# A graph network layer pair in one program: the expert rows transposed by a DMA from SBUF to SBUF instead of by TensorE

## The reference, cut to what matters

```python
logits = jnp.einsum('bsd,de->bse', input, Wg)
probs = jax.nn.softmax(logits, axis=-1)
top_vals, top_idx = jax.lax.top_k(probs, TOP_K)
...
h = jnp.einsum('ebsd,edh->ebsh', xm, W1) + b1[:, None, None, :]
h = jax.nn.relu(h)
y = jnp.einsum('ebsh,ehd->ebsd', h, W2) + b2[:, None, None, :]
out = jnp.sum(y * jnp.moveaxis(scores, -1, 0)[..., None], axis=0)
```

## Time and profile before

| | us |
|---|---|
| median of 3 runs | 2253.19 |
| lowest and highest of them | 2250.86, 2257.51 |
| the profiled execution, its span | 2275.1 |
| TensorE busy in it | 2087.9 (92%) |
| first work of the expert stage (first gather issued) | at 2065.9 |
| last accumulating write issued | at 2266.8 |

### The profile page before, as it was taken

The page is one execution under the profiler, slowest core; times in us unless marked ns, Lnnn a source line. Parts: engine busy times, 40 slices in busy tenths (PEclk is TensorE's granted clock), DMA queues, the critical chain, the costliest instruction groups (busy, mean ns, idle before and its releaser), DMA issues.

```text
span 2275.1 us, 41642 instructions
## 1 busy us (share of the span) xinstructions
PE 2087.9 (92%) x16528; PEld 1432.7 (63%) x16528; DVE 1235.5 (54%) x2230; ACT 752.7 (33%) x1097; POOL 1083.7 (48%) x797
## 2 busy tenths in 40 slices
PE   5969999999999989979999999999999998976997
PEld 5526446455447967754445577757887788874665
DVE  5871551554486789984634632545545534275332
ACT  4242453553564434440031322411211122051332
POOL 5456778678774420004621783025324425423554
PEclk9989999999999999988999999999999999987999
DMA  3311323232445420023000012300100000376886
GB/s 136 84 32 22 84 61 81 67 84 67 103 128 129 131 82 20 20 109 97 19 19 28 21 45 75 97 28 29 56 28 28 30 17 29 117 288 206 152 155 107
DMA packets 106982, 176.89 MB, mean 78 GB/s; under 512 B 31057, under 2 KB 76248, under 8 KB 100542
## 3 DMA queue, kind: packets, MB, share of 16 engines
q1 hardware_dynamic: 89966, 145.63, 20.4%
q0 software_dynamic: 16848, 28.90, 7.5%
HBM read 120.82 MB, written 53.49 MB: 77 GB/s over the span
## 4 chain that ended last, share of the span: by engine, by line
PE 77%; DVE 10%; issue 5%; POOL 4%; ACT 3%; DMA 2%; DVEq 0%; POOLq 0%; ACTq 0%; SPq 0%; another core or an unknown queue 0%
PE ps L487 19%; PE ps L489 19%; PE ps L490 19%; PE pt L697 4%; DVE RB L778 3%; PE ps L681 3%; PE pt L681 1%; PE pt L875 1%; ACT SR L740 1%; PE pt L1107 1%; PE ps L1126 1%; PE ps L1127 1%; PE ps L1128 1%; PE pt L472 1%; DVE RB L1760 1%
## 5 line engine op out<-in xcount | busy, mean ns | idle before, releaser
L487 PE MATMUL ps<-WR,RB 128*128 128x256 f16 (+2 forms) x2280 | 640.7, 281 | 11.0 <-POOL WR L1421 3.7
L489 PE MATMUL ps<-WR,RB 128*128 128x256 f16 (+2 forms) x2280 | 640.0, 281 | 0.1
L490 PE MATMUL ps<-WR,RB 128*128 128x256 f16 (+2 forms) x2280 | 639.7, 281 | 0.0
L487 PEld LDWEIGHTS ps<-WR,RB 128*128 128x128 f16 x2280 | 223.9, 98 | 58.5 <-issue 6.7
L1421 POOL TENSOR_TENSOR WR<-WR 128x2048 f16<-128x2048 f32 (+2 forms) x40 | 188.5, 4712 | 146.7 <-ACT WR L594 145.3
L487 PE MATMUL ps<-RB,WR 128*128 128x512 f16 (+1 forms) x720 | 244.4, 339 | 10.1 <-DVE RB L439 7.4
L490 PEld LDWEIGHTS ps<-WR,RB 128*128 128x128 f16 x2280 | 223.7, 98 | 43.6 <-issue 0.6
L489 PEld LDWEIGHTS ps<-WR,RB 128*128 128x128 f16 x2280 | 224.2, 98 | 41.1 <-issue 0.8
L490 PE MATMUL ps<-RB,WR 128*128 128x512 f16 (+1 forms) x720 | 244.3, 339 | 0.0
L489 PE MATMUL ps<-RB,WR 128*128 128x512 f16 (+1 forms) x720 | 244.3, 339 | 0.0
L1414 POOL TENSOR_TENSOR WR<-WR,units 128x3072 f32<-128x3072 f32 (+2 forms) x18 | 81.4, 4522 | 339.7 <-PE ps L487 334.7
(11 more groups left out here) (338 smaller groups left out, 4013.4 us busy)
## 6 DMA issues: line engine op xcount, KB each, us to landing
WR<-in_w_moe SPq DMA_DIRECT2D x64, 256.0 KB, 3.5
moe_split<-WR SPq DMA_DIRECT2D x128, 128.0 KB, 1.8
RB<-moe_split SPq DMA_DIRECT2D x8, 2048.0 KB, 13.7
WR<-in_w_mix SPq DMA_DIRECT2D x12, 1024.0 KB
WR<-in_w_mix SPq DMA_DIRECT2D x8, 1536.0 KB
RB<-in_x SPq DMA_DIRECT2D x18, 512.0 KB, 6.1
WR<-in_w_out SPq DMA_DIRECT2D x8, 1024.0 KB
RB<-counts SPq DMA_DIRECT2D x10, 640.0 KB, 4.8
```

The costliest lines, as they stand in the source:

```text
L487: m = nc.tensor.matmul(o, ah, bh, start=(k == 0), stop=False)
L489: nc.tensor.matmul(o, ah, bl, start=False, stop=False)
L490: m = nc.tensor.matmul(o, al, bh, start=False, stop=(k == n - 1))
```

## The change

TensorE no longer transposes the gathered rows, and ACT and DVE no longer copy them. In their place SP issues one transposing DMA a tile, from `xg` to `xT`, when the gather has landed and, from the fifth tile on, when `up` of the tile four before has read its buffer. `xT` gets four buffers. `pt`, which held the transposed rows, is used as a second set of banks for `up` and `down`, by odd and even tiles, so that both wait for the copy two tiles back instead of that of the tile before. The gather waits for the transposing DMA that read its buffer, where it waited for TensorE.

```diff
-        xT = [WR(24576 + 4096 * j, F16, 2, KD, 128) for j in range(2)]
+        xT = [WR(24576 + 4096 * j, F16, 2 * KD, 128) for j in range(2)] + [
+            SR(S1 + 8192 + 4096 * j, F16, 2 * KD, 128) for j in range(2)]
+        NX = len(xT)
...
+        def up_bank(t):
+            return (ps[:, 0, :] if t % 2 == 0 else pt[:, 0, 0, :])[:, 0:HE]
+
+        def down_bank(t, c):
+            return ps[:, 2 + c, :] if t % 2 == 0 else pt[:, 1, c, :]
...
-            def rows_turn(t):
-                pe.wait_ge(xg_loaded[t % NG], 16 * (t // NG) + 16)
-                if t >= 2:
-                    pe.wait_ge(xt_hi, t - 1)
-                    pe.wait_ge(xt_lo, t - 1)
-                for b in range(2):
-                    for k in range(KD):
-                        m = nc.tensor.transpose(pth[t % 2][:, b, k], xg[t % NG][:, b, k * 128:(k + 1) * 128], ident_h)
-                m.then_inc(xt_done, 1)
-
...
                 pe.wait_ge(blk_loaded[min(t, NE - 1)], 16)
-                pe.wait_ge(xt_hi, t + 1)
-                pe.wait_ge(xt_lo, t + 1)
-                if t >= 1:
-                    pe.wait_ge(u_hi, t)
-                    pe.wait_ge(u_lo, t)
+                pe.wait_ge(xt_loaded[t % NX], 16 * (t // NX) + 16)
+                if t >= 2:
+                    pe.wait_ge(u_hi, t - 1)
+                    pe.wait_ge(u_lo, t - 1)
...
-                if t >= 1:
-                    pe.wait_ge(y_out[c], t)
+                if t >= 2:
+                    pe.wait_ge(y_out[c], t - 1)
...
-            rows_turn(0)
             up(0, e)
-            rows_turn(1)
             hidden_turn(0)
             for t in range(MT):
-                if t + 2 < MT:
-                    rows_turn(t + 2)
                 if t + 1 < MT:
                     up(t + 1, e1)
...
-                nc.scalar.activation(xT[t % 2][:, 0], pth[t % 2][:, 0], ACT.Copy).then_inc(xt_hi, 1)
...
-                    pool.wait_ge(xt_done, t - NG + 1)
+                    pool.wait_ge(xt_loaded[(t - NG) % NX], 16 * ((t - NG) // NX) + 16)
...
             block_load(7)
+            for t in range(MT):
+                sp.wait_ge(xg_loaded[t % NG], 16 * (t // NG) + 16)
+                if t >= NX:
+                    sp.wait_ge(u_done, t - NX + 1)
+                sp.dma_start_transpose(out=xT[t % NX], in_=xg[t % NG].rearrange("p b n -> p (b n)")
+                                       ).then_inc(xt_loaded[t % NX], 16)
...
-                v.tensor_copy(xT[t % 2][:, 1], pth[t % 2][:, 1]).then_inc(xt_lo, 1)
```

More of the change, by code:

```diff
@@ L285, in build_program @@
         pt = ctx.enter_context(nc.psum_tensor("pt", [128, 2, 2, 512], F32))
-        pth = [pt[:, s, :, :].rearrange("p b c -> p (b c)").bitcast(F16).rearrange("p (b k n) -> p b k n", b=2, k=KD)
-               for s in range(2)]
         psh16 = ps[:, 1, :].bitcast(F16)
@@ L364, in build_program @@
         xg_loaded = [sem(f"xg_loaded{j}") for j in range(NG)]
-        xt_done, xt_hi, xt_lo = sem("xt_done"), sem("xt_hi"), sem("xt_lo")
+        xt_loaded = [sem(f"xt_loaded{j}") for j in range(NX)]
         u_done, u_hi, u_lo = sem("u_done"), sem("u_hi"), sem("u_lo")
@@ L1114, in up @@
                 pe.wait_ge(blk_loaded[min(t, NE - 1)], 16)
-                pe.wait_ge(xt_hi, t + 1)
-                pe.wait_ge(xt_lo, t + 1)
-                if t >= 1:
-                    pe.wait_ge(u_hi, t)
-                    pe.wait_ge(u_lo, t)
+                pe.wait_ge(xt_loaded[t % NX], 16 * (t // NX) + 16)
+                if t >= 2:
+                    pe.wait_ge(u_hi, t - 1)
+                    pe.wait_ge(u_lo, t - 1)
                 def w(at):
                     return WB[:, bass.ds(e, 1), at:at + HE].rearrange("p a n -> p (a n)")
-                o, x = ps[:, 0, 0:HE], xT[t % 2]
+                o, x = up_bank(t), xT[t % NX]
                 nc.tensor.matmul(o, pick_e[:, 0, t:t + 1].to_broadcast([128, 128]), b1s, start=True, stop=False)
                 for k in range(KD):
-                    nc.tensor.matmul(o, x[:, 0, k], w(k * HE), start=False, stop=False)
-                    nc.tensor.matmul(o, x[:, 0, k], w(2048 + k * HE), start=False, stop=False)
-                    m = nc.tensor.matmul(o, x[:, 1, k], w(k * HE), start=False, stop=(k == KD - 1))
+                    nc.tensor.matmul(o, x[:, k], w(k * HE), start=False, stop=False)
+                    nc.tensor.matmul(o, x[:, k], w(2048 + k * HE), start=False, stop=False)
+                    m = nc.tensor.matmul(o, x[:, KD + k], w(k * HE), start=False, stop=(k == KD - 1))
                 m.then_inc(u_done, 1)
@@ L1339, in up_hi @@
                     act.wait_ge(ht_done, t - 1)
-                nc.scalar.activation(hr[t % 2][:, 0], ps[:, 0, 0:HE], ACT.Relu, scale=1.0 / (XS * WS)).then_inc(u_hi, 1)
+                nc.scalar.activation(hr[t % 2][:, 0], up_bank(t), ACT.Relu, scale=1.0 / (XS * WS)).then_inc(u_hi, 1)
             def hidden_hi(t):
@@ L1352, in y_first @@
                     act.wait_ge(summed[0], 16 * (t - 2))
-                nc.scalar.activation(yo[t % 3][:, 0:512], ps[:, 2, :], ACT.Copy,
+                nc.scalar.activation(yo[t % 3][:, 0:512], down_bank(t, 0), ACT.Copy,
                                      scale=sc[:, t:t + 1]).then_inc(y_out[0], 1)
             act.wait_ge(sc_ready, 1)
-            rows_hi(0)
             up_hi(0)
-            rows_hi(1)
             hidden_hi(0)
             for t in range(MT):
-                if t + 2 < MT:
-                    rows_hi(t + 2)
                 if t + 1 < MT:
```

14 lines of the change are left out of this document (3 added, 11 removed).

## The result

| | before | after |
|---|---|---|
| median, us | 2254.78 (4 runs) | 2298.02 (4 runs) |
| lowest and highest, us | 2250.86, 2257.51 | 2288.23, 2318.29 |
| ratio, 95% interval | | 1.0207 [1.0178, 1.0235] |
| profiled execution: span | 2275.1 | 2296.7 |

The account below looks back on a forecast made before the run. TensorE bounds the expert stage at 6.956 us a tile, with DMA engines and writes next. 22 spacings of 7.15 us (157.3) + 23.6 - 178.4 + 3.5 for the start give +6.0 us: 2259 us, range 2235 to 2300.

Parts of the forecast that it names:

- the next limit: Expert loop: chain of accumulating writes has 0.05 to 0.7 us slack at 6.06 us a tile; existing DMA share 0.94.
- X: Time one tile's transposing DMA takes of each DMA engine: 2.23 us, bounds 1.24 and 3.14 us.
- The period after: Expert loop: time a tile lies between 6.06 us (gaps filled) and 7.93 us (no overlap); 7.15 us taken.
- P: Tile period of the expert loop while gathers and transposes run: 7.15 us; the change is nil at 6.88.
- The start: Start of expert stage: first transpose delays up(0), which runs at the low clock; +3.5 us (1.5 to 6).
- The sum: Expert stage: 22P + 23.6 - 178.4 + 3.5 us, which gives +6.0 us, a median of 2259 us.
- Rival 3: Expert loop: DMA times never overlap, period 7.93 to 8.84 us, +23 to +43 us, 2276 to 2296 us; chance 0.18.
- Rival 2: Expert loop: TensorE stays the bound, period 6.06 to 6.57 us, -18 us at 6.06, 2235 us; chance 0.32.
- Rival 4: SP's queue: transpose worked off block by block, 9.8 us a tile, +80 us, 2333 us; chance 0.08.
- The doubled banks: Expert loop, waits of up and down for a free bank: gain nothing at 6.06 us, as TensorE has no idle time.

Follow-up runs that it names:

- no gathers: Changed kernel with only the first five gathers, later tiles reusing those buffers; 2247.97 us, ratio 0.9973 to before.
- no writes: Changed kernel without the accumulating writes to the output and the waits for them; 2236.15 us, ratio 0.9919 to before.
- neither: Changed kernel with only the first five gathers and without accumulating writes; 2235.25 us, one execution.
- plain copy in 256 B pieces: Changed kernel with SP's transposing DMA replaced by two untransposed copies a tile in 256 B pieces; 2252.18 us, ratio 0.9997 to before.
- the two plain copies: Changed kernel with SP's transpose replaced by an untransposed copy, in 4096 B or 256 B pieces; 2250.36 and 2252.18 us.
- the collision: Transpose and gather issued 0.06 us apart, in the kernel before with every third tile from 5 on transposed by DMA; that kernel took 2271.88 us.

## Why the prediction was wrong

**What bounded the kernel, and the sign of the next limit**: right. TensorE gave up its 0.89 us a tile, and where the other DMAs were light (no gathers, no writes, neither) the period was 6.06 us, as worked out. The next limit was the chain of accumulating writes and the DMA engines, also as said. `up` also came to wait for its transpose, in 13 tiles.

**X, the transpose's time of each engine**: near by itself, but low. 2.23 us were taken from a line between two packet sizes; 2.6 us (20.6 ns a packet) and 2.7 us (21.4 ns) were measured with nothing beside it, within the bounds of 1.24 and 3.14. In the sum that is 22 x (2.7 - 2.23) = 10.3 us of the miss. The plain copy in 256 B pieces came to 128 x 18.4 ns = 2.36 us. The rate alone is 1.89 MB in 10 us, 189 GB/s. The Trainium skill (DMA: Bandwidth & Descriptors, Latency and other measured facts) has 261 GB/s in one kernel; the trace is slower, and the measurement decides.

**The period after**: this is the step that failed. It took P between 6.06 us (full overlap) and 5.70 + 2.23 = 7.93 us (none), and chose 7.15, so it let 0.78 us a tile overlap. The period was 8.51 us. With X as measured alone, the sum without overlap is 5.70 + 2.7 = 8.40 us, so on the mean of the loop nothing overlapped. The step treated X as a price that a packet has whatever lies beside it. A transposing packet had that price only alone: beside gathers and writes on GpSimd's queue a transposing packet took 34.0 ns, 4.35 us a tile, while the writes landed after 8.3 us in place of 5.2. For plain packets of the same size the step was even too dear: without overlap they would have needed 5.70 + 2.36 = 8.06 us, and their period was 6.62 us. The warning was in the prediction's own rows (a gather among writes cost 1.88 us in place of 1.43, "mixing has made work dearer here"), but it was used to lean inside the interval and not to question its upper end. In the sum it is 22 x (8.50 - 7.15) = +29.7 us, 8.50 being the P with which 22P + 23.6 gives the measured 210.6: 10.3 us for X alone, 22 x 0.78 = 17.2 us for the overlap that did not come, and 2.2 us above the sum without overlap.

**The start**: right in kind, mis-sized. 3.5 us (1.5 to 6) were forecast and 13.4 measured, +9.9 us. `up(0)` did run at the low clock level, as said (its products 0.21 us apart from 2062.22 on, and the granted clock 0.50 from 2042 to 2062, in which TensorE had nothing to do). The miss is the transpose beside gathers 1 to 4: X was added once more for the sharing, and it landed after 16.1 us. Some of it is the price of any copy in this place: the two plain copies had `up(0)` 5.0 and 6.4 us later than before, the transpose 13.0.

**The sum.** 6.0 + 29.7 + 9.9 + 0.5 for the tail is 46.1 us, the measured difference of the stages; on the medians it is 43.

**The rivals.** Rival 3 (nothing overlaps, 2276 to 2296 us, chance 0.18) came nearest. Its range of periods, 7.93 to 8.84 us, holds the measured 8.51, and with X = 2.7 its sum gives 8.40; the time of 2298.02 us lies above its range only because of the start. It has no reason for why plain packets do overlap, and it holds for the mean alone: the collision took 18.2 us for 9.4 us of work, and at the start the 20.6 us from 2041.44 to 2062 had only five gathers and 0.73 MB of transposing in them, 5 x 1.43 + 1.39 x 2.7 = 10.9 us by their prices alone. Rival 2 would have needed a landing of about 5.7 us. The plain copy in 256 B pieces had just that, and still gained nothing, because 22 x (6.96 - 6.62) = 7.5 us less in the loop were given back at the start (+6.4 us). Rival 4 is out: SP's queue puts out a transpose in 1.8 to 4.6 us, the first two apart (2.3 with the engines to itself), far from 9.8, though also far from the 0.3 to 0.6 that was expected. Inside the loop no row shows that length as a cost, as nothing else was on the queue, but at the start it held back transposes 2 to 4.

**The doubled banks** were to gain nothing; no run tests them apart, so this stays unshown.

**What stays open.** Why some transposing packets take so long beside GpSimd's DMAs, and why those land late then. That plain packets don't suffer is shown, and so is that writes alone are company enough. That it needs two queues is not shown: in every kernel with dear packets gathers or writes were on GpSimd's queue, also in the one that brought the loads on SP's. What the engines do in that time is not in the trace. It is also open which of gathers and writes is the worse partner in the loop; the collision and the start had a gather in them. No kernel here that does all of the work beats the one before.

## What to carry to other kernels

A price that a transposing DMA has alone was no price beside other DMAs here: before moving work from a busy engine to the DMA engines, put the new DMA into the old kernel with nobody reading it, and look at the period. That one run (+50 us) would have told the sign and the size. For a transposing stream beside gathers and accumulating writes, take the sum of the works without overlap (8.40 us here, 8.51 measured) as the expected period and not as its upper end, for single collisions took twice their sum; and a high DMA share says little (1.09 at 233 GB/s and at 182 GB/s), so read it with the bytes a second and the time of a packet.

## What the runs showed of the hardware

- A transposing packet of 256 B from SBUF to SBUF took 20.6 to 21.4 ns alone, 24.1 beside gathers, 26.4 beside writes, 34.0 beside both, and 69 ns at the start of the stage beside a burst of gathers. These are means; most such packets take 18 ns in company too, and a few take up to 1.56 us. A plain one of that size took 18.4 ns beside gathers and writes. The Trainium skill (Advanced Engine Details and Errata, X-Bar Transpose (TRN2)) says that transpose DMAs are as fast as regular ones: for packets of equal size the traces nearly agree as long as the transpose is alone (20.6 against 18.4 ns), in company they don't (34.0), nor against a plain copy in 4096 B pieces, which took 20.0% x 6.71 = 1.34 us of each engine a tile where a transpose alone took 2.6 to 2.7.
- One transpose and one gather issued 0.06 us apart landed together, after 18.2 and 17.7 us; in the middle 10 us of it the engines moved 89 GB/s.
- While a transpose is in such company SP's queue is held too: 15.79 us for two beside gathers, against 4.7 for the next two.
- Accumulating writes of 256 KB landed after 5.2 us, after 5.7 beside plain copies and after 8.3 beside transposes and gathers, while the packets of their queue took no longer (187 ns on the mean after the change, 212 before, 2100 to 2200).
- The granted clock fell in the loop, from 1.00 to 0.92 on the mean, since TensorE now waits: after the idle 4.25 us ahead of 2098.05 the products of `up` are 0.22 us apart (the 1.2 GHz level), where they were 0.11 at 2087.57. That deepens a stall but is no cause of it, as far as the runs show: with plain copies in 256 B pieces, where TensorE waits less, it kept 1.00.
